# A multi-stage recurrent-memory and routing kernel issues its 1005 steps in another order

## What is computed

```
k, v, q = causal_conv4(x @ Wk.T), causal_conv4(x @ Wv.T), causal_conv4(x @ Wq.T)
alpha, eta, theta = means over channels of sigmoid, sigmoid, softplus of x @ (aW, eW, tW).T
for each chunk of 128 tokens:
    g = grad of |silu(k W1.T) W2.T - v|^2 at the W of the chunk's start, times 0.1, norm clipped to 1
    S = eta S - theta g;   W = (1 - alpha) W + S          # token by token
    out = silu(q W1.T) W2.T                               # with the W of the token
out = rmsnorm(out @ Wo.T) * norm_g * (x @ gW.T + gb)
x = layernorm(x + out)
e = argmax(x @ gate_w.T);   x = layernorm(x + x + expert_w[e] @ x)
```

## Time and profile before

| what | value |
|---|---|
| median of 3 runs | 583.77 us (579.64 to 592.17) |
| span of the profiled execution, first to last instruction | 546.5 us |
| around the span, against the median | 37.3 us |
| PE busy | 461.7 us (84%) |
| DVE, ACT, POOL busy | 385.6, 339.1, 332.0 us |
| matmuls | 3702 |

### The profile page before, as it was taken

The page is one execution under the profiler, slowest core; times in us unless marked ns, Lnnn a source line. Parts: engine busy times, 40 slices in busy tenths (PEclk is TensorE's granted clock), DMA queues, the critical chain, the costliest instruction groups (busy, mean ns, idle before and its releaser), DMA issues.

```text
span 546.5 us, 11654 instructions
## 1 busy us (share of the span) xinstructions
PE 461.7 (84%) x3702; PEld 358.3 (66%) x3702; DVE 385.6 (71%) x1125; ACT 339.1 (62%) x834; POOL 332.0 (61%) x457
## 2 busy tenths in 40 slices
PE   4678989999988998989989999888788578775993
PEld 2356757867857675767858786656667466564883
DVE  3356984978689887696897986979576446543562
ACT  1357556786776665767676768674457356742673
POOL 2005165265495846789677797567337776666677
PEclk9798899999999999999998999999779798987898
DMA  8324424643536273536656354557754647346652
GB/s 216 103 81 115 119 59 108 157 105 92 146 99 179 57 189 76 155 69 156 170 101 170 79 162 113 130 126 232 166 136 107 183 140 207 116 155 212 193 150 69
DMA packets 64140, 73.76 MB, mean 135 GB/s; under 512 B 20078, under 2 KB 50991, under 8 KB 64081
## 3 DMA queue, kind: packets, MB, share of 16 engines
q1 hardware_dynamic: 53408, 46.65, 31.6%
q0 software_dynamic: 8848, 25.44, 18.0%
q10 hardware_dynamic: 1824, 0.93, 0.7%
HBM read 44.20 MB, written 19.22 MB: 116 GB/s over the span
## 4 chain that ended last, share of the span: by engine, by line
PE 34%; DVE 22%; POOL 13%; ACT 12%; issue 9%; DMA 6%; SPq 3%; POOLq 0%; ACTq 0%; DVEq 0%
PE bank L1225 8%; DVE kq_in L543 7%; POOL sorted_rows L1010 5%; PE bank L589 4%; PE bank L502 4%; ACT rows L943 3%; PE bank L520 3%; PE bank L1202 2%; DVE grad_w L794 2%; DVE y L914 2%; DMA hq<-hq 2%; DMA front<-in_hidden_t 2%; DMA sorted_rows<-rows,index 2%; PE bank L950 2%; POOL rstd L935 2%
## 5 line engine op out<-in xcount | busy, mean ns | idle before, releaser
L1264 POOL DMA_INDIRECT out<-os,xs_token x71 | 70.2, 988 | 32.1 <-issue 12.6
L1010 POOL DMA_INDIRECT sorted_rows<-rows,index x64 | 69.7, 1089 | 30.0 <-POOL index L1006 13.7
L543 DVE SCALAR_TENSOR_TENSOR kq_in<-shared,conv_w,kq_in 128x256 f32<-128x256 f32 x144 | 70.1, 545 | 11.7 <-ACT kq_in L537 11.6
L1225 PE MATMUL bank<-shared,front 128*128 x280 | 74.4, 413 | 2.0 <-issue 1.9
L502 PE MATMUL bank<-front 128*64 128x256 f32 x512 | 63.2, 398 | 13.9 <-DMA bias_t<-in_bias_t 7.5
L589 PE MATMUL bank<-front 128*128 128x256 f32 x256 | 62.2, 390 | 1.7 <-DVE kq L670 1.7
L1225 PEld LDWEIGHTS bank<-shared,front 128*128 128x128 f32 x280 | 55.3, 208 | 11.2 <-issue 3.7
L502 PEld LDWEIGHTS bank<-front 128*64 128x64 f32 x512 | 36.1, 142 | 34.6 <-DMA bias_t<-in_bias_t 7.5
L589 PEld LDWEIGHTS bank<-front 128*128 128x128 f32 x256 | 47.6, 194 | 9.2 <-DVE kq L670 2.1
L1259 ACT ACTIVATE os<-bank,rs 128x256 f32<-128x256 f32 x70 | 35.7, 560 | 19.0 <-DVE rs L1248 17.2
L914 DVE SCALAR_TENSOR_TENSOR y<-bank,rms,gt 128x256 f32<-128x256 f32 x64 | 26.5, 476 | 26.8 <-POOL rms L910 12.5
(11 more groups left out here) (211 smaller groups left out, 1249.3 us busy)
## 6 DMA issues: line engine op xcount, KB each, us to landing
front<-sorted_rows SPq DMA_DIRECT2D x71, 130.0 KB
front<-in_hidden_t SPq DMA_DIRECT2D x16, 512.0 KB, 5.0
decay<-gate_clear SPq DMA_DIRECT2D x16, 512.0 KB, 4.1
y<-in_hidden POOLq DMA_DIRECT2D x16, 512.0 KB, 5.6
q<-kq_in SPq DMA_DIRECT2D x64, 64.0 KB
carry<-carry_rows SPq DMA_DIRECT2D x32, 128.0 KB
hq<-hq SPq DMA_DIRECT2D x64, 64.0 KB
w<-state SPq DMA_DIRECT2D x32, 64.0 KB, 2.8
```

The source lines that it names most:

```text
L543: dve.scalar_tensor_tensor(dst, raw[g][:, kind, :, tap:tap + P], conv_w[:, kind, tap:tap + 1], dst, ALU.mult, ALU.add))
L1010: pool.indirect_dma_start(sorted_rows[:, :], bass.IndirectOffsetOnAxis(index[i2][:, b:b + 1], 0), R[:, b, :], None, bounds_check=NE * REGI ...
L1225: ins = pe.matmul(both[:, i, :], xs_t[t % TURNED][:, i, k, :], w_expert[:, k, bass.ds(expert, 1), :], start=k == 0, stop=k == KH - 1)
L1264: pool.indirect_dma_start(out[:, :], bass.IndirectOffsetOnAxis(xs_token[t % LOADS][:, i:i + 1], 0), os_[o][:, i, :], None, bounds_check=TO ...
```

## The change

The diff:

```diff
--- before.py
+++ after.py
@@ -1285,23 +1285,23 @@
 
 
 ORDER = (
-    "p0p0p0p1p0p0p1p0p0p0p0p0p0p0p2l0p1p1p1p1p1p1s0p1l0l0l0s0l0p1p1l0l0l0s0s1s1p3s0p1l0l1p2p2p2s0l0s1p4p2p2s0p2p2l1l1r0l1p2p2"
-    "p2s0r0l1p2s1l1r0s2s2l1l1l1s1s2l2p3p3p3l1s2l2p3p3s1l2p3r0p3r1e0e0s2l2e0s1p3l2p3p3p5l2p7r0l2s3l2r1l2s3p3l3r1l2p4p4p4p4s2l3"
-    "p4p4r1l3p4p4p4p4r2l3s2r1s3e0l3p4e0r0p8s4l3e1r2s3s4s3e0l3r2e1p5p5l3r1p5e1l3l4l3e0e1p5p5p5p5s3r2e0p5e0l4e0s3s4p9p5p5p6e1r3"
-    "e2l4r2l4p5s4l4s4s5e0s4e0l4r3l4e2e1l4r3s5p6l4e2p6p6l5p6e0p6p6e1p6r3l5p6l4r2l5e1e2l5e0p6s4e0e1p6l5e1s6e2e1p6r4l5s5r3s5e3p7"
-    "e1l5s5e3e2r4l5r4p7s6e3p7e1e1p7l5p7r4s5l6l5e3p7p7s5p7e1p7p7l6l6e2s6r5e4r3l6s7s6p7l6r4e3l6l6e4e3par5s7p8e4p8r5s6e2s7s7p8e2"
-    "e2e2s6p8l6e2r5l6p8e3s6p8l7r4p8s7e3e2p8l6l7e3e3e4p8l7pbl7p8e2e2r6e3l7e4r5l7p8l7s8r6e5r6e5e4p9p9p9e3s8l7s8l7e3e5p9p9l8e5l7"
-    "p9s7e4s7p9r6p9e3e4l8p9e3l8e4e4l8r7s8s8e5p9l8e4r6l8l8r7e6p9e4e6s9l8r5e5e4pal8pas9e6s9r7l9e5l8pas9pas8s8e6e4e4papas9r7l9pa"
-    "e5r8e5l9l9e5pae5papas9r6e6l9e7l9pasae7e5l9e6l9r7l9s9e7r8lae5pbpbsar8e7lal9e5e5lapbsasapbpbr8lae7r7pde6pbpbpcr9r8lae8lapb"
-    "sblae8lapblapbsar9e7r9e8lbpbsbpce6sblapce6e6lbe6sae6e8e6pcsae6lbe6lbpcpcsbpcr8pcr9lbe8e7pcrae9pelbsce9lbe8pclbr9e9rapcsb"
-    "pdlbsbscrae7scpce7e7e7sclcpde7lbsbe8pfpdlce9r9e7e7e7lce8lcpde8e8rbe9ralcpde8pdpdearalce8scealce9rbeae8lcrbpdlcpde9ldrbe9"
-    "ealcsdldpdsdsce8e9e9peebe8ldsdldpde9sdldeae9ebrcpeldscealdebpee9peldperbldrapeebpeearcpee9lde9earceapepeeasdrcsdeblerdec"
-    "eaeasesdebsepeleecrbsepfleecpfeceaserdpfeaealerdpfpfeblepfpfebecleebebebrcleseleebeblew0pflfecrdleebebsfy0sfedy0lfedy0se"
-    "y0y0pfrepfedy0lfrdlfsfpfw0x0relfedreeclfresfx0x0w0edeelfx0x0x0eesfedx0eelfx0y0eex0lflfx0x0x0x0ecx0ecx0ecx0x0ecedx0x0sfx0"
-    "x0x0x0x0ececx0ededx0x0ecededecedx0rfx0eex0edrfx0rfedx0edx0x0x0sex0eex0x0x0rfx0x0efx0x0efefx0x0rcefx0x0x0x0x0sfx0x0x0x0m0"
-    "x0x0x0eem0x0x0x0x0x0x0x0x0eeefx0x0eex0x0x0x0x0m0x0m0efx0x0x0x0eex0efx0x0efeex0x0x0m0efm0efx0eeefx0x0x0eeeeefx0eeefx0efx0"
-    "x0m0x0x0x0x0z0x0z0x0x0efx0x0x0x0x0x0x0x0z0rfx0z0z0z0z0z0x0x0x0x0x0x0x0x0x0x0x0x0x0x0x0rfx0x0x0x0x0x0x0x0x0x0x0x0x0x0x0x0"
-    "x0x0x0x0x0x0x0x0x0x0x0x0x0x0x0x0x0x0x0x0x0x0x0x0x0x0x0x0x0x0x0x0x0x0rex0x0x0rdx0x0x0rex0x0"
+    "p0p0p0p0p0p0p2p0p0p0p0p0l0p1p0p1p1p1p1p1s0p1p1l0s0l0l0p1l0s0l0l0l0s0p1l0p1s1s1l1p1s0l0s1l1p2p2l1p2p2s1p2p2l1p2p2p2p2s0p4"
+    "l1l1p2s0l1s2l1l1s1r0s1p3l2r0r0l2p3s2s2l2l1s2p3p3l2p3s2p3s1p3p3l2r0l2l2p3r0s2r1p3s2p5l2l2p3r1s3l3e0r1p3l3s3s3p4l2p4s3p4e0"
+    "l3s3e0l3p4p4p4p4r1p4s3l3r1l3r0r2e0l3s3l3s4p4l3p4p6e0r2s4e1l3r2e1l4p4p5s4e0p5p5e1p5e1r2p5p5p5r1l4p5e0r3l4e0l4e0p5e1l4e0s5"
+    "r3p5l4e0r2e0e1s4s4l4e2e2l4r3s5e0p5l4s5e2l5l4p6e2p6p6p6p6r3p6p6p6e1l5s4p6l5p6r2e0l5s4e1p7l5p6e0l5e1l5s5e1r4r3l5e2s6e3r4e2"
+    "e1e1s5r4l5s6l6e3p7p8e1e3p7l5p7p7p7s5p7r4p7l6e2p7r3e1s6l6e3p7l6e1s5p7s6r5e3e2r4l6e2r5p7l6e2s7r5e4s6e2p8e3e2p8s7e2e4s7l6s7"
+    "e4p8l6l6l7s7p8p8l6p8e4p8p9e3l7pap8e2e3s6r5l7l7s6e2e4r4p8e3p8r6r5e3l7e5l7l7p8e5e3r6l7s8e3e4s8e5l7l7p9p9p9e3l8p9e5p9r6s7p9"
+    "p9p9pbp9p9l8e4s7l8r7l8e3e3e4r6p9s8e4r5e4e5r7l8s9s8e6e6e4e4s8l8s9e4r6l8e5l8e6l8papapal9r7pae6l8papapae5pal9e4pae5l9l9s8pa"
+    "s8e5e4e5s9s9r7r8e5l9e5e6s9e7sar7r6l9pae5e7pbr8l9e6sapbpbl9e7l9e7pbpblar8pbpbpbe6pbl9pclas9e5r8e5sae6sas9lalae6e6pbe6e6r9"
+    "r8lasae8e7r7lapblasbr9e8e7sbe8pcpcsapcr9lapcpclae6lalbpcpcpce7r9e8sapdpee7pclbpce7e7e6sblbe6e7sclbsbr8e7rasbe9e9e8pclbr9"
+    "lbe7e8pdlblbpdrasce9pdlbpdpdralce7lbpdpdpdpdpdlce8e9ralcsbsbe8lce7e9rbe8sdrarblcr9scpde8e8sclcsdearblceasdlce9sde8lcpepe"
+    "eae8pescscperbpepepepflde9lcpeeae8e8peldlde9sclde9e9eapercldrbldsdrcebsee9sde9ebseldldpeeae9sepfsdpfldebpflde9rcebpfpfe9"
+    "pfpfearardlerceaw0leealelerbeaeaebleecleebseecpfleearcrdealeecrdecebleleeaeaseebsfseebebeblfrdebebsflfebecy0y0edeceblfsf"
+    "sfpfy0y0lfrepfy0edrdlfedy0pfedw0ecrerew0ecx0lfy0ececresfedx0x0eex0lfx0eeecx0x0x0x0lfx0x0lfx0x0x0sex0x0ecx0ecx0edx0sflfx0"
+    "x0x0x0x0eeeex0x0rfrex0ecedecx0rfrfx0ededx0ededx0rfx0eex0efefedx0x0x0x0x0edx0eeefx0efx0x0x0x0x0x0x0x0eex0x0edx0x0edx0x0x0"
+    "eex0x0x0x0x0eex0efeex0x0eeeex0eex0x0x0x0x0x0x0m0m0x0x0m0m0x0eeefx0x0x0m0x0x0efm0eex0x0x0x0x0efx0m0x0x0efefefx0efefx0efx0"
+    "x0rcx0x0efx0x0rex0x0z0z0x0x0x0x0x0sfx0x0x0x0x0x0x0x0x0z0rfz0z0z0x0z0rdz0x0x0x0x0x0x0x0x0x0x0x0x0x0x0x0x0x0x0x0x0x0x0x0x0"
+    "x0x0x0x0x0x0x0x0x0x0x0x0x0x0x0x0x0x0x0x0x0x0x0x0x0x0x0x0x0x0x0x0x0x0x0x0x0x0x0rfx0x0x0x0x0"
 )
 
 
```

## The result

The new order takes 589.24 us (median of 4 runs, 585.46 to 592.62) against 583.54 us (median of 4 runs of the old order, 579.64 to 592.17, measured beside it): ratio 1.0138, 95% interval 1.0077 to 1.0200. It is a little slower, on the other side of zero from the forecast of 579, though inside the range of 566 to 595.

A forecast was written before the change was run, and what follows sets the result against it. It took PE to pace the items until 350 us and POOL the stretch from the first send. Terms 0 + 2 - 6 + 4 - 4.5 = -4.5 us on a 546.5 us span, plus 37.3 around it, gave 579; range 566 to 595.

The forecast's parts named there:

- The items: 50 to 350 us: longer waits on h against ended waits on onehot, +2 us, bounds -3 to +8.
- the signs named: Signs to check among the items: PE's busy share from 50 to 350 us, waits on h grown, those on onehot gone.
- the waits on onehot: Among the items, e.12 to e.13 gets more PE work between, which should end these waits, 2.8 us.
- the waits of l.1 on h: Among the items, too little PE work between l.0 and l.1 in five items; waits on h grow.
- The start: 0 to 50 us: PE stands about as long for scaled gate weights; 0, bounds 1.4 us lost, 3.7 won.
- Before the first send: 350 to 411.6 us: earlier expert weights and fewer steps from load0 to send0; 6 us won, bounds 0 and 9.
- Experts: Up to 489 us: POOL idles around load7 and ef.1; 4 us lost, bounds 0 and 10.8.
- tail: Last sends: load23 ahead of the eight pad tiles closes POOL's holes; 4.5 us won, bounds 0 and 5.3.
- both holes: POOL's waits of 2.58 and 2.25 us before sends 21 and 22 in the tail, forecast to close.
- the rival through SP's queue: Experts: load7 slips behind rf's hq and re.4's state, POOL idles 10.8 us; +8.3, 592 us; chance 0.20.
- its point: Experts: the loss passes 2.5 us when load7 goes more than 1.5 us after ec.14's scatters end.
- The 37.3 us "around the span": Whole kernel: difference between the profiled span of 546.5 and the median of 583.77, left unchanged in the forecast.

The follow-up runs named there:

- r3: New order up to the first table of tiles (713 steps), then the remaining steps in the old order; 593.00 us, ratio 1.0396 to the old order.
- r1: Old order run again unchanged, with its profile; 576.96 us, ratio 1.0115 to the old order.
- r12: New order run again unchanged, as measure for two mended orders; 585.94 us, ratio 1.0110 to the old order.
- r16: Old order up to the first table of tiles, new behind it, r4's order run again; 577.06 us, ratio 0.9821 to the old order.
- r9: New order with s0.4, l0.9, s1.2, l1.1, l1.2 put behind p2.1 to p2.3 as in the old order; 590.12 us, no ratio formed.
- r11: New order with only item 6's position and scatter steps (e6.13, e6.14) moved earlier; 585.79 us, ratio 1.0128 to the old order.
- r5: New order with position and scatter steps of items 0 to 7 and 9 to b 2 to 21 places earlier; 608.50 us, 1.1155 of the old order.
- r6: Old order with position and scatter steps of items 0, 1, 2, 4 to 7 10 to 17 places later; 588.02 us, 1.0749 of the old order.
- r4: Old order up to the first table of tiles (712 steps), then the remaining steps in the new order; 570.43 us, ratio 0.9990 to the old order.
- r2: New order run again unchanged, with its profile; 583.81 us, ratio 1.0238 to the old order.
- r18: Old order with the four wide products of every item moved from POOL to DVE; 551.07 us, ratio 1.0095 to the old order.
- r7: New order for 540 steps, old up to the first table of tiles, new behind it; 557.35 us, ratio 1.0268 to the old order.
- r8: Old order for 540 steps, then new to the end; 553.65 us, ratio 1.0166 to the old order.
- r17: New order with the four wide products of every item moved from POOL to DVE; 561.62 us, ratio 1.0252 to the old order.

## Why the prediction was wrong

**The items (the step that failed).** The forecast had +2 us, bounds -3 and +8. r3 measured 15.0 us for all steps up to the table; by work done it is 12.9 us at 300 us of work, 10.5 without the start. The sum of PE's idle time between 50 and 350 us doesn't show it: 22.8 us in the page before, 25.7 in r1 and in the page after alike. The working counted, for two kinds of pairs, whether enough PE work lies between a step and its answer, and took PE as the pace. Of the signs named, the waits on onehot did go. But the waits of l.1 on h shrank from 5.9 to 3.1 us, and others grew that had not been counted, such as l.4's on the error. PE's waits between 50 and 350 us, page after, then page before:

```profile
PE bank L749 <- DVE grad L742: 7.7, 4, 3.8
PE bank L723 <- DVE h L716: 3.1, 2, 2.1
PE bank L990 <- DVE y L914: 2.5, 1, 2.5
```

```profile
PE bank L723 <- DVE h L716: 5.9, 5, 2.0
PE bank L749 <- DVE grad L742: 3.0, 3, 1.4
```

The working also had no term for the clock, which at 300 us of work had cost 4.7 to 7.2 us in three traces of the old order and 11.3 to 15.4 in three of the new; r12 (new, 7.9) and r16 (old, 16.5) show that it varies as much within one order.

Single distances didn't show what sets the pace: r9 and r11 mended single ones and gained nothing, r5 and r6 moved one kind of step and lost 36 to 40 us. What exactly in the new order costs the 10 us is open; the surest 5 to 6 of them fall between 260 and 300 us of work. It isn't the one hole, nor item 6's scatter, nor POOL's wide products alone. A calculation of all five queues together, or hybrids finer than two halves, would be needed.

**The start (0, bounds -3.7 and +1.4).** PE waits 4.8 us for the scaled gate weights (L324) as foreseen. At 20 us of work the new order stands at 37.0 us on average and the old one (page before, r1, r4) at 34.6: +2.4, past the bound. Over all twenty traces it is 36.6 to 38.3 us with the new start and 32.0 to 36.3 with the old. The forecast went by weights that are ready at 20.63; in r1 they are ready at 22.9 and in the page after at 22.7. In r1 the 16 matmuls of p1.1 (1.95 us there) stand inside that wait, and in the new order they come behind it.

**Before the first send (-6, bounds 0 and -9): right in size, and half of the reason is shown.** The cleanest pair is r4 and r1: one chip, the same order up to step 712, and eb's scatter ends at 392.5 and 392.7. The first sends:

```profile
412.40 1.14 POOL L1264 DMA_INDIRECT out<-os,xs_token  x1 [1.32 <-ACT front L1205]
```

```profile
418.97 1.66 POOL L1264 DMA_INDIRECT out<-os,xs_token  x1 [0.83 <-ACT front L1205]
```

That is 6.6 us won. (From the end of eb's scatter the first send takes 26.2 and 26.3 us in the page before and r1, 19.1 and 19.2 in the page after and r2, but in the whole new order eb.14 also stands seven places later.) From load0 to the first send it is 13.5 us against 16.9: this half is what the forecast expected of fewer steps between them. The other half comes ahead of load0, and it doesn't need the moved weights: in r4 they stand at their old place, right ahead of the round trip, which is back after 3.7 us:

```profile
378.93 1.27 SPq L1135 DMA_DIRECT2D shared<-in_w_expert  x2
...
385.58 0.30 SPq L647 DMA_DIRECT2D keep_rows<-keep_t  x1
389.31 1.13 SPq L652 DMA_DIRECT2D carry<-carry_rows  x2
```

The Trainium skill (DMA: Bandwidth & Descriptors, Queues, rings and completion order) has each DMA engine take the descriptors of SP's row in ring order. The traces agree: with the weights right ahead the round trip is back 10.1, 9.4 and 9.1 us after SP has issued them (page before, r1, r4), though it was issued itself 4.2, 4.0 and 5.4 us behind them; with the weights some 12 us ahead or more it takes 1.9 to 2.3 us (page after, r2, r3).

**Experts (+4) and tail (-4.5).** Behind the end of ef's scatter the new order has 37 sends left and the old one 35, and two sends are 2.6 us, so I take the last 35 sends as the tail. On the chips where the old order takes 545 or 546 us, and in the page before, the last 35 sends take 48.2, 45.3 and 45.1 us with the old order behind the table (page before, r6, r18) and 43.4, 43.9, 44.5 and 45.4 with the new (r7, r8, r5, r17). Against the page before, from which the forecast was made, the 4.5 us are there, and for the reason given: load23 comes ahead of the pads, and both holes are closed. In r7 each of the last 35 sends goes 0.30 us behind the one before it, and in r8 (at 0.30 or 0.31) all but one:

```profile
516.03 0.97 POOL L1264 DMA_INDIRECT out<-os,xs_token  x1 [0.63 <-DVE mvs L1234]
...
549.25 0.97 POOL L1264 DMA_INDIRECT out<-os,xs_token  x1 [0.30 <-issue]
```

Over the three old traces it is 1.9 us, since the holes are smaller in r6 and r18. From the first send to the first of the last 35 it is 84.6, 86.1 and 85.4 us against 83.1, 83.6, 84.3 and 83.5: 1.7 us won and not 4 lost. In the page after, load7 went 3.1 us before ec's scatter had ended, so the rival through SP's queue never came near its point. On the slower chips nothing of this is left: from the first send to the last it is 153.0 and 152.3 us in the old order (r1, r3) and 153.4, 154.5 and 151.2 in the new (r4, page after, r2).

**The 37.3 us "around the span".** There are 2 us around it. As an addend it did no harm, since the median stayed where it was; as a reading it did, since the tail was read in an execution without the stalls that the timed runs have (below). The loads and pads had been laid out against 8.84 us of pads that take 13 to 16 in those.

**The sum.** With the terms of the slower chips, where the change was timed, it is 2.4 + 10.5 - 6.6 + 0 = +6.3 us, and the whole change measured +5.7 to +6.9 us by medians in three comparisons. That it fits so well is partly luck, as traces of one order lie up to 10 us apart at 300 us of work (343.4 in r4, 353.1 in r16), and on the faster kind r18 and r17 differ by 13.6 us there and by 15.0 at the first send, so the 6.6 can't be seen in that pair. That the time still fell inside the stated range is luck too: an item term 8 to 13 us too low stood in a range of 29 us. A slip without weight: 35 x 1.29 is 45.15 and not 45.0.

## What to carry to other kernels

When an order of many steps changes on several in-order queues, don't stop at summing single waits: compare how much work is done by a time, as busy time times granted clock, and split the rest into idle and clock. A busy share that stays the same can hide a slower pace (here a hundred matmuls fewer). Change an order in parts that meet at a point where all engines wait anyway; here one part was worth 7 us and the other cost 15. And before a profile is read, see whether its span is near the median; if it isn't, it shows another case than the one that is timed.
